# An expert matrix folded into the routed projection, and reordered steps in a two-block adaLN kernel

## The reference, cut to what matters

```python
# block 0, second half: "first MLP"
logits = h @ gate_w; routing_weights, _ = top_k(logits, 2)
shared_out = relu(h @ up_w) ** 2 @ down_w              # 512 -> 1024 -> 512
x_latent = h @ fc1_w                                   # 512 -> 256
expert_out = x_latent @ expert_w                       # 256 -> 256, linear
moe_out = expert_out * sum(routing_weights)
x = x + gb * layernorm(shared_out + moe_out @ fc2_w, gamma, beta)
# block 1, first half: "mixer", at sequence length 1: the shifted scans are zero, the convolution has one tap
mid = gelu(h @ w_down.T + b_down)                      # 512 -> 128
for y in range(2):                                     # hydra, twice
    z, xs = split(src @ in_w.T); xs = silu(xs * w + b)
    yz = xs * (xs @ fcD_w.T + D) * silu(z)
    src = yz * rsqrt(mean(yz ** 2) + eps) * norm_w @ out_w.T
x = rest(x) + ga * (alpha-mix of mid and src) @ w_up.T
# block 1, second half: "second MLP"
x = x + gb * (silu(h @ W1.T) * (h @ W3.T)) @ W2.T       # 512 -> 1376 -> 512, W = w + 2 * B @ A
```

## Time and profile before

| | |
|---|---|
| Median of 3 runs | 810.98 us |
| Profiled execution, its own time | 809.74 us |
| Its span | 807.7 us |
| TensorE busy | 732.0 us (91%) |
| VectorE busy | 480.2 us (59%) |
| ScalarE busy | 323.1 us (40%) |
| GpSimd busy | 337.8 us (42%) |
| Mean granted clock of TensorE | 0.968 |

### The profile page before, as it was taken

One profiled execution on the slowest core, in us unless ns is written; L12 is line 12 of the kernel. 1 busy time (PEld: TensorE's weight loads), 2 busy tenths in 40 slices (PEclk: granted clock), 3 DMA queues, 4 the chain that ended last, 5 costly groups with the idle time before them and its releaser, 6 DMA issues.

```text
span 807.7 us, 10131 instructions
## 1 busy us (share of the span) xinstructions
PE 732.0 (91%) x3654; PEld 440.6 (55%) x3654; DVE 480.2 (59%) x715; ACT 323.1 (40%) x536; POOL 337.8 (42%) x277
## 2 busy tenths in 40 slices
PE   4897999889999999879999999799778999997998
PEld 2443333333343332148678888454447788875886
DVE  3758777677778776246565457767785333336311
ACT  3311266566766766751245311454243333222100
POOL 0227993785475553671165332213532222124300
PEclk9998899999999999999999999999789999998999
DMA  9442624150550500230033200213000110111111
GB/s 312 151 116 68 141 79 90 68 115 15 102 108 10 115 3 2 95 99 7 0 83 100 65 1 1 72 43 65 34 6 27 53 52 26 52 52 52 40 66 39
DMA packets 24110, 52.99 MB, mean 66 GB/s; under 512 B 4252, under 2 KB 8100, under 8 KB 23044
## 3 DMA queue, kind: packets, MB, share of 16 engines
q1 hardware_dynamic: 24068, 52.44, 23.7%
HBM read 45.63 MB, written 6.60 MB: 65 GB/s over the span
## 4 chain that ended last, share of the span: by engine, by line
PE 68%; DVE 12%; issue 8%; POOL 6%; ACT 3%; DMA 1%; SPq 1%; ACTq 0%; DVEq 0%; POOLq 0%
PE ps L862 65%; DVE mxp L1755 3%; PE ps L879 2%; ACT pr L1411 1%; DMA rq<-in_mask 1%; POOL wsum L2165 1%; DVE st L1597 1%; POOL pr L2181 1%; POOL x L2275 1%; DVE xnb L1621 1%; DVE x L1943 1%; DVE arena L1640 1%; PE ps L1028 1%; POOL wmr L2163 1%; POOL rs L2094 1%
## 5 line engine op out<-in xcount | busy, mean ns | idle before, releaser
L862 PE MATMUL ps<-arena 128*128 128x512 f32 (+1 forms) x1416 | 332.1, 395 | 7.9 <-DVE arena L1640 4.2
L862 PEld LDWEIGHTS ps<-arena 128*128 128x128 f32 (+1 forms) x1416 | 264.8, 188 | 68.2 <-DVE arena L1640 6.1
L1755 DVE TENSOR_REDUCE mxp<-ps 128x2 f32<-128x1024 f32 (+3 forms) x160 | 172.6, 1114 | 55.0 <-PE ps L862 53.3
L1411 ACT ACTIVATE pr<-ps 128x512 f32<-128x512 f32 x288 | 162.3, 596 | 86.5 <-PE ps L862 84.0
L862 PE MATMUL ps<-Qst,Kst 99*128 99x512 bf16 x288 | 103.0, 388 | 9.5 <-ACT pr L1411 7.4
L862 PE MATMUL ps<-Kst,Qst 96*128 96x512 bf16 (+3 forms) x384 | 101.5, 336 | 7.6 <-DVE mxp L1755 5.8
L2181 POOL TENSOR_TENSOR pr<-pr,cap 128x512 int32<-128x512 int32 x56 | 70.7, 1278 | 32.8 <-ACT pr L1411 32.6
L862 PE MATMUL ps<-pr,vr 128*32 128x512 f32 x576 | 76.8, 606 | 5.0 <-POOL pr L2181 4.3
L862 PEld LDWEIGHTS ps<-Kst,Qst 96*128 96x128 bf16 x384 | 35.8, 99 | 66.3 <-DVE mxp L1755 26.8
L862 PEld LDWEIGHTS ps<-Qst,Kst 99*128 99x128 bf16 x288 | 26.6, 98 | 82.3 <-ACT pr L1411 60.9
L2280 POOL TENSOR_TENSOR arena<-raw,arena 128x1024 fp32r<-128x1024 f32 x11 | 27.1, 2467 | 84.3 <-ACT arena L1477 84.3
(11 more groups left out here) (197 smaller groups left out, 821.2 us busy)
## 6 DMA issues: line engine op xcount, KB each, us to landing
wmr<-in_wmr SPq DMA_DIRECT2D x8, 1280.0 KB, 11.3
raw<-in_w SPq DMA_DIRECT2D x16, 512.0 KB, 3.3
Qst<-q_parts SPq DMA_DIRECT2D x42, 128.0 KB
q_parts<-qparts SPq DMA_DIRECT2D x3, 768.0 KB, 3.7
x<-in_x SPq DMA_DIRECT2D x8, 256.0 KB, 6.4
wm<-in_wm SPq DMA_DIRECT2D x4, 512.0 KB, 7.4
raw<-in_up SPq DMA_DIRECT2D x8, 256.0 KB, 2.6
raw<-in_down SPq DMA_DIRECT2D x8, 256.0 KB, 2.6
```

The lines of the kernel that those rows point to most:

```text
L862: return nc.tensor.matmul(outp, lhs, rhs, start=start, stop=stop, skip_group_check=True)
L1411: A(pr[:, k % PRING, :], ps[:, 4 + k % 2, :], ACT.Exp, scale=float(DH) ** -0.5).then_inc(exp_done, 1)
L1755: V.tensor_reduce(mxp[:, kh, g0:g0 + heads, i].rearrange("p (b e) -> p b e", e=per), units, AXX, ALU.max)\
```

## The change

- The expert matrix is transposed on TensorE (`expertT`), split, and multiplied into fc2 (`routed_w`, two jobs of 6 matmuls between the turn of the second half and its gate). `routed` then takes the latent directly, and the four `eo` jobs go.
- fc2 is loaded before the up loop and split by GpSimd behind Wo's last tile; the first up piece is split before the low parts of the second half.
- The first Wo tile begins with the products of high parts. VectorE takes four low parts of `aT` before `modT`.
- In the MLP's tile loop the first half's statistics are finished in turn 4, not 5. Shared tile 0 starts before the last chunk of products is ready.
- Three tiny activations (`load_table`) make the activation table be loaded ahead of the first Gelu, the first Silu and the second Gelu.
- In the mixer `centred`, `rest` and `shift` of the second half come earlier; the second w13 piece is split beside the first, ahead of the last `out` on GpSimd. `dg`, `rb` and `Wuo` move to other addresses for it.
- Two of the four normalised tiles of the third norm's first half are written by VectorE.
- The floor of `gb1` is computed before the loop of the second MLP. Four w2 pieces, not two, are merged before the last gated chunk's products; `lora2` 4 to 6 stand before the first chunk of down, 7 to 10 before chunks 1 to 4.

```diff
-MIXER_DVE = [("fd", 0, 0), ("rows", 0, 0), ("dg", 0, 0), ("scale", 0, 0), ("fd", 0, 1), ("centred", 0, 0), ("dg", 0, 1),
-             ("fd", 1, 0), ("scale", 0, 1), ("centred", 0, 1), ("merge", 0, 0), ("dg", 1, 0), ("rest", 0, 0),
-             ("fd", 1, 1), ("scale", 1, 0), ("rest", 0, 1), ("dg", 1, 1), ("up", 0, 0), ("scale", 1, 1), ("up", 0, 1),
-             ("up", 1, 0), ("up", 1, 1)]
-MIXER_POOL = [("out", 0, 0), ("wup", 0, 0), ("out", 0, 1), ("shift", 0, 0), ("out", 1, 0), ("shift", 1, 1),
-              ("w13", 0, 0), ("out", 1, 1)]
+MIXER_DVE = [("fd", 0, 0), ("rows", 0, 0), ("dg", 0, 0), ("scale", 0, 0), ("fd", 0, 1), ("centred", 0, 0),
+             ("centred", 0, 1), ("dg", 0, 1), ("fd", 1, 0), ("scale", 0, 1), ("rest", 0, 0), ("merge", 0, 0),
+             ("rest", 0, 1), ("dg", 1, 0), ("fd", 1, 1), ("scale", 1, 0), ("dg", 1, 1), ("up", 0, 0), ("scale", 1, 1),
+             ("up", 0, 1), ("up", 1, 0), ("up", 1, 1)]
+MIXER_POOL = [("out", 0, 0), ("wup", 0, 0), ("out", 0, 1), ("shift", 0, 0), ("shift", 0, 1), ("out", 1, 0),
+              ("w13", 1, 1), ("out", 1, 1)]
...
+        if t == 1:
+            banks.add("expertT")
...
+            for kc in range(2):
+                banks.add(("routed_w", kc))
...
-    for hf in range(2):
-        for m in range(2):
-            banks.add(("eo", hf, m))
...
+    pieces.add("fc2")
     pieces.loop([("up", 0), ("down", 0), ("up", 1), ("down", 1)], HC0 // 2)
-    pieces.add("fc2")
...
-        dg = at("dg", [P, 4, P], F32, WR_B + 8 * 1024)
-        rb = at("rb", [P, HALF], F32, WR_B + 10 * 1024)
+        dg = at("dg", [P, 4, P], F32, HT_B + 26 * 1024)
+        rb = at("rb", [P, HALF], F32, HT_B + 28 * 1024)
...
-        Wuo = at("Wuo", [P, D], F32, WR_B + 12 * 1024)
+        Wuo = at("Wuo", [P, D], F32, HT_B + 24 * 1024)
...
-            pe.wait_ge(s_read, ctx_at(NKV - 1) + 2)
+            pe.wait_ge(s_read, ctx_at(NKV - 1) + 1)
...
             b = bank_of(pe, "modT")
             nc.tensor.transpose(ps[:, b, 0:40], full[0:40, 1, 0:P], ident[0:40, 0:40]).then_inc(full_b[b], 1)
+            pe.wait_ge(s_read, ctx_at(NKV - 1) + 2)
...
-                if t % 4 == 0:
+                b = bank_of(pe, ("wo", t))
+                if t == 0:
+                    for kc in range(KC):
+                        pe.wait_ge(sp_hi, kc + 1)
+                        mm(ps[:, b, :], aTr[0][:, kc, tl(t)], Wo[0][:, kc, :], kc == 0, False)
+                        mm(ps[:, b, :], aTr[0][:, kc, tl(t)], Wo[1][:, kc, :], False, False)
+                    for kc in range(KC):
+                        evacuated(pe, ("aT", 0, kc))
+                        last = mm(ps[:, b, :], aTr[1][:, kc, tl(t)], Wo[0][:, kc, :], False, kc == KC - 1)
+                    last.then_inc(full_b[b], 1)
+                    continue
+                if t == 4:
                     for c in range(KC):
-                        evacuated(pe, ("aT", t // 4, c))
-                b = bank_of(pe, ("wo", t))
...
+                if t == 1:
+
+                    s = raw_loaded(pe, "expert")
+                    b = bank_of(pe, "expertT")
+                    for m in range(2):
+                        for kc in range(2):
+                            last = nc.tensor.transpose(ps[:, b, LAT * m + P * kc:LAT * m + P * kc + P],
+                                                       raw[:, s, LAT * kc + P * m:LAT * kc + P * m + P], ident[:, :])
+                    last.then_inc(full_b[b], 1)
...
                     ln_turn(1, 1)
+                    evacuated(pe, "expertT")
+                    weights(pe, "fc2")
+                    for kc in range(2):
+
+                        b = bank_of(pe, ("routed_w", kc))
+                        for m in range(2):
+                            last = mm3(ps[:, b, :], hilo(WexT, lambda w: w[:, m, kc * P:(kc + 1) * P]),
+                                       hilo(Wf2, lambda w: w[:, m, :]), m == 0, m == 1)
+                        last.then_inc(full_b[b], 1)
...
-            weights(pe, "expert")
-            for hf in range(2):
-                for m in range(2):
...
-            pe.wait_ge(pr_lo, 2 * HC0)
+            pe.wait_ge(pr_lo, 2 * HC0 - 2)
             for t in range(NT):
                 if t == 0:
-                    weights(pe, ("down", 1), HC0 // 2 - 1)
+                    weights(pe, ("down", 0), HC0 // 2 - 1)
...
                 for kc in range(HC0):
+                    if t == 0 and kc == HC0 - 1:
+                        weights(pe, ("down", 1), HC0 // 2 - 1)
+                        pe.wait_ge(pr_lo, 2 * HC0)
...
                 last.then_inc(full_b[b], 1)
+                if t == 0:
+                    for kc in range(2):
+                        evacuated(pe, ("routed_w", kc))
                 if t % 4 == 0:
                     for m in range(2):
-                        evacuated(pe, ("eo", t // 4, m))
-                if t == 0:
-                    weights(pe, "fc2")
+                        evacuated(pe, ("fc1", t // 4, m))
...
-                    last = mm3(ps[:, b, :], hilo(eo, lambda h: h[:, kc, tl(t)]), hilo(Wf2, lambda w: w[:, kc, :]),
+                    last = mm3(ps[:, b, :], hilo(lat, lambda h: h[:, kc, tl(t)]), hilo(Wf2, lambda w: w[:, kc, :]),
...
-            for k in range(W2_AHEAD, W2_AHEAD + 4):
-                lora2(k)
-            for q in range(1):
-                for c in range(HC1):
-                    if W2_AHEAD + 4 + c < HC1:
...
+            for c in range(HC1):
+                for k in {0: (4, 5, 6), 1: (7,), 2: (8,), 3: (9,), 4: (10,)}.get(c, ()):
+                    lora2(k)
+                if c in (0, HC1 - 1):
+                    pe.wait_ge(pr_lo, 2 * HC0 + 2 * (HC1 - 1 if c == 0 else HC1))
+                weights(pe, ("w2", c // 2))
+                for t in range(4):
+                    down(0, c, t)
...
+                if hf:
+
+                    filled(act, ("routed_w", 1))
+                    for kc in range(2):
+                        split_hi(("routed_w", kc), Wf2[0][:, kc, :])
...
+            def load_table(kind, k):
...
+                A(unused[:, k:k + 1], eps[:, :], kind)
...
             act.wait_ge(eps_ready, 1)
+            load_table(ACT.Gelu, 0)
...
                     A(midf[:, tok[hf]], ps[:, b, :], ACT.Gelu, bias=cols[:, C_BD:C_BD + 1]).then_inc(read_b[b], 1)
+                    if hf == 0:
+                        load_table(ACT.Silu, 1)
...
+                    if (y, hf) == (0, 0):
+                        load_table(ACT.Gelu, 2)
...
-                    w13_hi(("w13", 0), 0, ("lora3", "F", 0))
+                    for k in range(2):
+                        w13_hi(("w13", k), k, ("lora3", "F", k))
...
-                for t in range(4):
+                for t in range(4 if hf else 2):
...
             ln_norm(0)
-            filled(act, ("wup", NT - 1))
-            w13_hi(("w13", 1), 1, ("lora3", "F", 1))
...
-            for c in range(2):
+            for c in range(W2_AHEAD):
                 w2_hi(c)
             gate_unit(0, ("E", 0), HC1 - 1)
-            for c in range(2, W2_AHEAD):
-                w2_hi(c)
...
+            for c in range(KC):
+                split_lo(c, ("aT", 0, c), aTr[0][:, c, tok[0]], aTr[1][:, c, tok[0]])
             b = filled(dve, "modT")
...
-            n = 0
-            for hf in range(2):
-                for c in range(KC):
-                    split_lo(n, ("aT", hf, c), aTr[0][:, c, tok[hf]], aTr[1][:, c, tok[hf]])
-                    n += 1
+            for c in range(KC):
+                split_lo(KC + c, ("aT", 1, c), aTr[0][:, c, tok[1]], aTr[1][:, c, tok[1]])
+            n = 2 * KC
...
-                if t >= 2:
+                if t >= 2 and t != 5:
                     dve.wait_ge(x_mlp, t - 1)
                     ln_stat((t - 2) // 4, (t - 2) % 4)
+                if t == 4:
+                    dve.wait_ge(x_mlp, t)
+                    ln_stat(0, t - 1)
+                    ln_finish(2, 0)
                 if t == 5:
-                    ln_finish(2, 0)
                     ln_norm(2, 0)
...
+                    if (y, hf) == (1, 0):
+                        dve.wait_ge(ln_nb, 1)
+                        filled(dve, ("ln", 2, 1, KC - 1))
+                        for t in range(2, 4):
+                            V.tensor_scalar(xnb[:, t, :], x[:, t, :], rs[:, 0, t:t + 1], nb[:, 0, t:t + 1], ALU.mult,
+                                            ALU.add).then_inc(ln_xn, 1)
...
+            dve.wait_ge(gb1_in, 16)
+            floor_gate(gb1[:, :], gb1t[:, :]).then_inc(gb1_ready, 1)
+            dve.wait_ge(gb1_ready, 1)
             with dve.Fori(0, HC1 // 2 - 1) as i:
                 for j in range(2):
                     merge(("w13", "L", j), [("lora", "L", j), ("lora3", "L", j)], i)
                     gate_unit(i, ("L", j), 2 * i + 2 + j)
-            dve.wait_ge(gb1_in, 16)
-            floor_gate(gb1[:, :], gb1t[:, :]).then_inc(gb1_ready, 1)
-            dve.wait_ge(gb1_ready, 1)
...
-            for c in range(2):
```

(40 more changed lines are left out.)

41 lines of the change are left out of this document (11 added, 30 removed).

## The result

The changed kernel takes 785.04 us (median of 4 runs, 782.99 to 786.61) against 811.5 for the kernel before on the same chip: a ratio of 0.9673, 95% interval 0.9646 to 0.9699. A second measurement of it gave 783.9 (5 runs) and 0.9659 (0.9634 to 0.9685). The profiled execution has a span of 782.4 us, 25.3 less than before, and a time of 784.32.

The account below looks back on a forecast made before the run. TensorE, busy 91% of the span, was taken as the bound, with holes and the low clock behind them costing extra. Six terms summed to -25.6 us, from 809.74 to 784.1, put at 785; range 777 to 795, likeliest 780 to 790.

Parts of the forecast that it names:

- (a): First MLP: eo jobs removed, routed_w added, holes and clock dip before the up loop gone; -7.4 us, bounds -4 to -8.
- (b): First half's norm statistics a tile earlier, so VectorE starts xnb sooner; -1.8 us, bounds 0 and -3.0.
- (e): Layer norm before the second MLP: two xnb tiles to VectorE, w13 low part moved away; -2.3 us, bounds 0 and -4.
- (c): Activation table loads ahead of use; in starts 1.3 us earlier but xnb caps the gain; -0.5 us, bounds 0 and -1.3.
- (d): Mixer: rest terms before fd(1,1), so yz starts 4.1 us earlier; -7.0 us in all, bounds -2 and -9.5.
- (f): Start of down: lora2 8 no longer waits for VectorE's merge, clock dip gone; -6.6 us, bounds -3 and -7.
- with both holes the dip behind them: Before the first MLP's up loop: filling both TensorE holes also removes 3.4 us of low clock, worth 1.7 us.
- the strict reading: Mixer: by the SBUF exclusion rule both rest groups take 5.8 us, and (d) gives about 3 us less.
- R1: Rival: GpSimd takes VectorE's place in the mixer, both out steps late, (d) gives 2 and (e) 0.5; 792 us, chance 0.15.
- R4: Rival: slower, the clock stays low through the mixer between 520 and 612 us; 815 us, chance 0.04.
- R2: Rival: all waits re-form and low stretches stay, only TensorE's own work goes, 2.2 us; 808.5 us, chance 0.04.
- R3: Rival: holes filled beyond the count, w13 low parts hidden, low stretches all gone; 778 us, chance 0.13.

Follow-up runs that it names:

- n_mlp: The kernel before with all of the change except the first MLP's part (expert output computed as before); 789.13 us, ratio 0.9727.
- u_up: The changed kernel with the first up piece's split back behind the second half's low parts and the last fc1 job; 787.86 us, ratio 0.9701.
- u_half: The changed kernel with all four normalised tiles of the third norm's first half on ScalarE; 783.11 us, ratio 0.9645.
- u_lora2: The changed kernel with lora2 4 to 8 ahead of down's first chunk and the W2 merges placed as before; 788.52 us, ratio 0.9717.

## Why the prediction was right, step by step

The time (785 against 785.04) and the sum of the steps are right. One reason in (a) and sizes in (a), (b) and (e) were not. That the time is met to 0.04 us is luck: the errors of the terms cancel, two measurements of the changed kernel differ by 1.1, and the span also has 0.6 us more ahead of the change. Rows of before against those of after, counted between marks of one profile, each from where the one above ends:

| step | predicted | measured | what differed |
|---|---|---|---|
| (a) first MLP | -7.4 | -7.7 | 5.5 + 1.4 (clock) + 0.8 (holes less added work, 0.2 predicted) |
| (b) statistics | -1.8 | -2.4 | GpSimd's addition held one step of VectorE, not the `xnb` |
| (c) table loads | -0.5 | -0.4 | |
| (d) rest terms | -7.0 | -7.2 | dg(1,1) -6.2, norm behind it -1.0 |
| (e) last norm, to the first `lora3` of the second MLP | -2.3 | -2.1 | more before the second turn, nothing behind it |
| (f) start of down, to its second chunk | -6.6 | -6.7 | |
| the rest of down | 0 | +0.6 | two `lora2` that moved behind this mark |
| sum | -25.6 | -25.9 | with 0.6 more ahead of the change: -25.3 of span |

(a) The reason given for 1.7 us, "with both holes the dip behind them", doesn't hold. `n_mlp` has both holes and no low clock, `u_up` one hole and the low clock. Between the two profiles shown it came to 1.4, but it isn't a property of this part: by `n_mlp` the part is worth 6.2 us up to the mixer and 5.2 (by the medians) in the end. The step that failed is the one that charged a low stretch to the holes ahead of it. The 0.3 us charged for a late up split didn't come.

(b) I took 1.3 us for GpSimd's `bb` addition against VectorE. It did hold VectorE's last step of the norm of a tile (1.66 us), but `xnb` then ran free, 1.90 us for four tiles against 2.84 in the earlier trace rows, and TensorE's wait went to 0.60.

(d) "5.75 beside GpSimd" held for the first rest group (5.95); the second took 2.73 (predicted 2.8), since GpSimd was through by then. So the strict reading, which would have given 3 us less, wasn't tried here: its condition, both groups beside GpSimd, never came. The terms behind `yz` were right too: 2.8 + 5.5 + 1.0 + 0.1 = 9.4 predicted, 570.35 - 561.16 = 9.2 measured. What I hadn't priced: the low parts held VectorE's `hof` for 2.35 us, hidden behind the wait for the root.

(e) was nearly right in sum and wrong in both parts. The time from the first tile to the second turn fell by 2.1 us (12.54 to 10.45), where I had 1.5. Of that I had counted 1.4 for the two tiles on VectorE, which `u_half` shows to be worth nothing; that leaves the w13 low part, gone from the stretch, though no run moved it alone. Behind the second turn I had 0.8 for the clock and got nothing: "the next turn is at the full clock, or half of it" was wrong in both profiles of the changed kernel, with sixteen transposes in 3.57 and 3.46 us, where 1.9 is the full level. The kernel before was low there too (its timeline):

```profile
609.12 3.18 PE L879 MATMUL ps<-ident,xnb 128*128 128x128 f32 x16
```

(f) Predicted were 4.5 for the start and 2.1 for the clock. The waits fell from 0.19 + 4.25 to 0.41 us, by 4.0, and the first twelve matmuls of down from 5.04 to 3.01, which is 2.0 of clock. The other 0.6 of the 6.7 are mostly two `lora2` that now stand behind the mark, and they come back in the row below. The twelve matmuls in the kernel before:

```profile
741.91 5.04 PE L862 MATMUL ps<-arena 128*128 128x512 f32 x12
```

In `u_lora2` the same twelve took 4.44 us, so the same order paid 1.4 for the clock and not 2.0. Here too the wait is the sure part.

R1 did not come. With the 9.9 us by which everything stands earlier at this point, the prediction had GpSimd at its eight additions from 545.4, done at 557.8, and the first `yz` at 561.2; the rows have 545.40, 557.95 and 561.16. R4 is refuted by the mean clock of 0.98 between 520 and 596. R2 would have needed the waits again; those on `yz`, the up split and `lora2` are gone or down to 0.7 us. R3 needed the w13 low parts hidden and no low stretch; they hold the last root until 569.31, and one stretch is left.
